# Last layer's dispatch: experts chosen in two parts, the choice in fewer operations, two gated products moved behind the logits

## The chip, the cores and the metric

The kernel runs on one core of one Trainium2 chip. Its time is the device time of one execution in microseconds; the time of a kernel is the median of its runs. The engines are TensorE (PE in the rows), VectorE (DVE), ScalarE (ACT), GpSimd (POOL) and SyncE (SP). Each works through its own list of instructions in order, and they wait for each other by semaphores.

## The reference, cut to what matters

Two layers over 4096 tokens of width 256 are computed, each an attention-like part and a mixture of experts, with a modulation by fixed vectors around them. Layer 0's mixture runs two rounds ("B0", "B1") with 6 experts of which each token takes 2; layer 1's ("D") is what the change is mostly about:

```python
h = _layernorm(x, axis=-1) * (1 + cb) + sb
# _L1_ffn_ref(h, ...), 8 experts, 2 per token
t = h * rsqrt(mean(h * h) + 1e-6) * norm_weight
gate_logits = t @ gate_w.T
gate_scores, expert_idx = top_k(gate_logits, 2)
routing_weights = softmax(gate_scores)
out = sum over the two experts of routing_weight * (gelu(t @ W1.T + B1) @ W2.T + B2)
x = x + gb * (h + out)
```

## The kernel before

The tokens are eight tiles of 512 (`NB = 8`, `CT = 4` groups of 128 rows each, 32 groups in all: `NT`). Every order below is the order in which the program text issues instructions to an engine.

**Preparation of layer 1's mixture** (`d_prep_*`). For each tile VectorE takes statistics (`d_stats_vector`, L2273 and L2277), GpSimd the inverse deviation (`rs`, a small filler L183, L2332 and a power L2334), VectorE the modulated row in two passes of four operations (`d_modulate_vector`, L2288, which does not need `rs`, and L2292, which does), ScalarE the sum of squares (`d_squares_scalar`, L2358), GpSimd the inverse root mean square (`rs2`, L183, L2342, L2344), TensorE the transposed rows (`turned`, L2393), ScalarE their copy out of PSUM (`take`, L2368, into one of two buffers `p_hT`), TensorE the logits (`logits`, L2402) and the product with the gate vector's diagonal (`gated`, L2412), VectorE the scaled logits (L2312) and the addition of the gated product to x (`d_residual_vector`, L2304), ScalarE the normalised rows (`rows`, L2376), which SyncE stores to DRAM (L2431).

VectorE works three tiles ahead: in turn t it does the modulation of tile t+3, the statistics of tile t+4, the addition of tile t-1 and the logits of tile t. GpSimd's order is rs(0), rs(1), rs(2), rs2(0), rs(3), rs2(1), rs(4), rs2(2), rs(5) and so on. `rs2(t)` has a wait of its own:

```python
if t >= 2:
    g.wait_ge(r.logits.sem, r.logits.at(t - 2))
```

because the two buffers that it writes are read by the scaled logits.

**Choice** (`routed_vector`, L952 to L987): over all 32 groups at once VectorE picks the best expert and then the second, 8 operations for the first and 10 for the second, each waiting for the one before. The second starts with three that take the first pick out of the logits (L968, L970, L972). In layer 0 the same function is used with 6 experts. The sum of the picks goes to `picked` (L2443 for layer 1, L1771 for layer 0), with a transposed write.

**Dispatch** (`dispatch_vector`, `dispatch_tensor`): TensorE counts the picks, VectorE works out each token's slot, then builds one-hot tables in four quarters (L2489 to L2492) whose product on TensorE (L2519) inverts the permutation; from it VectorE makes the row numbers for the gathers (L2495 to L2504). GpSimd then gathers rows (L2571) and scatters results (L2577) while TensorE multiplies for 39 blocks of 256 slots (L2618, L172). The one-hot tables lie where the preparation's buffers lay, so their start waits for the last gated product and the last stored rows.

**In layer 0's rounds** the second choice, `picked` and the ranks are VectorE's work between the rounding steps of the expert products (L1651, L1658, L1664, L1667), and TensorE's transposition of a later tile waits for the ranks (`COUNT_AT`).

Of the kernel before, what the change touches and what calls it, by code (L numbers as in the profile page):

```python
# [14 lines left out]
P = 128  # L15
# [936 lines left out]
def routed_vector(v, b, link, kind, which):  # L952

    E = E1 if kind == "D" else E0
    g = b.logits[:, :, 0:E]
    z, t, one, two = (x[:, :, 0:E] for x in (b.r_z, b.r_t, b.r_one, b.r_two))
    top = b.r_top[:, :]
    rank = mid(b.rank[:, 0:E], NT)
    if which == 0 and kind == "D":
        v.tensor_copy(z, g).then_inc(link.sem, 1)  # L960
        v.wait_ge(link.sem, link.next())
    elif which == 0:
        row = ROW["gb"] + (kind == "B1") * E0
        v.tensor_tensor(z, g, mid(b.rows[:, row:row + E0], NT), ALU.add).then_inc(link.sem, 1)
        v.wait_ge(link.sem, link.next())
    pick, gate = ((one, b.r_ga[:, :]), (two, b.r_gb[:, :]))[which]
# [7 lines left out]
    v.tensor_reduce(top, z, AX.X, ALU.max).then_inc(link.sem, 1)  # L974
    v.wait_ge(link.sem, link.next())
    v.tensor_tensor(t, z, spread(top, E), ALU.is_equal).then_inc(link.sem, 1)
# [7 lines left out]
    v.tensor_tensor(t, pick, g, ALU.mult).then_inc(link.sem, 1)  # L984
    v.wait_ge(link.sem, link.next())
    v.tensor_reduce(gate, t, AX.X, ALU.add).then_inc(link.sem, 1)
    v.wait_ge(link.sem, link.next())  # L987
# [1319 lines left out]
def d_prep_vector(v, b, s, r):  # L2307
# [9 lines left out]
    for t in range(NB):  # L2317
        if t + EARLY < NB:
            d_modulate_vector(v, b, r, t + EARLY)
        if t + EARLY + 1 < NB:  # L2320
            d_stats_vector(v, b, r, t + EARLY + 1)
        if t >= 1 and t + 1 < NB:
            d_residual_vector(v, b, r, t - 1)
        logits(t)


def d_prep_gpsimd(g, b, r):
# [20 lines left out]
    for t in range(NB):  # L2348
        rs2(t)
        if t + EARLY < NB:  # L2350
            rs(t + EARLY)

# [8 lines left out]
def d_prep_scalar(act, b, s, r):  # L2361
    def take(t):
        par = t % 2
        if t >= 2:
            act.wait_ge(r.gh.sem, r.gh.at(t - 2))
        for k in range(KD):
            act.wait_ge(r.hT_ps.sem, r.hT_ps.at(t, k + 1))
            act.activation(b.p_hT[par][:, k, :], b.bank[k][:, :], ACT.Copy).then_inc(r.hT.sem, 1)  # L2368
# [12 lines left out]
    for t in range(NB):  # L2381
        take(t)
        rows(t)
        if t + 2 < NB:
            d_squares_scalar(act, b, r, t + 2)


def d_prep_tensor(pe, b, r, m):
# [7 lines left out]
    def logits(t):  # L2396
# [3 lines left out]
        for c in range(CT):  # L2400
            for k in range(KD):
                ins = pe.matmul(b.bank[4 + t % 2][:, c * E1:(c + 1) * E1], b.p_hT[t % 2][:, k, c * P:(c + 1) * P], b.router["D"][:, k, :],  # L2402
                                start=k == 0, stop=k == KD - 1)
        ins.then_inc(r.logit_ps.sem, 1)

    def gated(t):
        if t >= 2:
            pe.wait_ge(r.xh.sem, r.xh.at(t - 2))
        for c in range(CT):
            for k in range(KD):  # L2410
                at = (c % 2) * D + k * P
                ins = pe.matmul(b.bank[d_sum_banks(t)[c // 2]][:, at:at + P], b.p_hT[t % 2][:, k, c * P:(c + 1) * P], b.p_diag[:, k, :], start=True, stop=True)  # L2412
            if c % 2:
                ins.then_inc(r.gh.sem, 1)
# [6 lines left out]
    for t in range(1, NB):  # L2421
        turned(t)
        gated(t - 1)
        logits(t)
    gated(NB - 1)


def d_prep_sync(sp, b, r, rows):
    for t in range(NB):
        sp.wait_ge(r.hn.sem, r.hn.at(t))  # L2430
        sp.dma_start(rows[t * TB:(t + 1) * TB, :].rearrange("(c p) n -> p c n", p=P), b.p_xn[t % 2][:, :, :]).then_inc(r.row_kept[t % 2].sem, 16)  # L2431
# [5 lines left out]
def dispatch_vector(v, b, s, link, r, E, nblk):  # L2437
# [45 lines left out]
    for par in range(2):  # L2483
        v.wait_ge(r.row_kept[par].sem, r.row_kept[par].at(NB // 2 - 1))
# [17 lines left out]
    v.tensor_scalar(b.gather_i, b.gather_i, N - 1, None, ALU.bitwise_and).then_inc(r.gather_at.sem, 1)  # L2502
    v.wait_ge(link.sem, link.next())
    v.scalar_tensor_tensor(b.scatter_i, b.source, -1.0, b.padding, ALU.add, ALU.add).then_inc(r.scatter_at.sem, 1)  # L2504


def dispatch_tensor(pe, b, r, E, nblk):
# [4 lines left out]
    pe.matmul(b.bank[1][:, 0:E * NT], b.every, flat_picked, start=True, stop=True).then_inc(r.counted.sem, 1)  # L2512
    for j in range(4):
# [759 lines left out]
```

## Time and profile before

| | |
|---|---|
| median of 3 runs | 1962.32 us (1961.79 to 1965.76) |
| profiled execution | 1967.77 us, its span 1965.8 us |
| busy: TensorE, VectorE, ScalarE, GpSimd | 1747.9, 1392.4, 1026.4, 783.0 us |
| mean granted clock of TensorE over the span | 0.949 of full |
| preparation of layer 1's mixture, from the last addition of the part before to the last scaled logits | 1588.0 to 1628.7 us |
| choice and dispatch, to the first gather | 1628.8 to 1660.3 us |
| products of the 39 blocks | 1667.7 to about 1910 us |

Times in rows count from the start of the span. A row of the timeline has the start, the time from the first instruction's start to the last one's end, engine, line, operation, what is written and read, how many, and in brackets the idle time before it with what ended that. Instructions of an engine overlap by some 0.07 to 0.1 us, so the distance of two starts is what an operation costs in a row of operations.

### The profile page before, as it was taken

What the parts mean: (1) busy time and instruction counts of PE and PEld (TensorE: products, weight loads), DVE (VectorE), ACT (ScalarE), POOL (GpSimd) and SP (SyncE); (2) the same over time, 40 slices, a digit from 0 to 9 for tenths busy, and PEclk for the clock granted to TensorE, in tenths of its full rate; (3) what the DMA queues carried; (4) which work ended last, traced back from release to release, by engine and by line L of the source; (5) the groups of instructions that cost most, each with busy time, mean ns of one, the idle gap of its engine ahead of it and who ended that gap; (6) DMA issues with size and microseconds to landing.
All of it is one profiled execution on the core that took longest, in us unless ns stands there. A gap on an engine that the chain in (4) does not pass through costs nothing.

```text
span 1965.8 us, 31803 instructions
## 1 busy us (share of the span) xinstructions
PE 1747.9 (89%) x11154; PEld 1543.5 (79%) x11154; DVE 1392.4 (71%) x2536; ACT 1026.4 (52%) x2052; POOL 783.0 (40%) x860
## 2 busy tenths in 40 slices
PE   5999999999999999999969999999289984999990
PEld 4788888888888878888858788888166784999990
DVE  4665465465445788777758887777699897788876
ACT  4344344334322434555546446554488653888882
POOL 2132232232222101777731037777222041788840
PEclk9899999999998999999978999999699986999995
DMA  4200000000012430666753326666710013788948
GB/s 161 65 1 12 11 0 11 11 11 0 11 58 65 129 126 20 205 198 193 204 185 118 116 63 208 191 197 172 232 65 1 1 63 139 255 268 271 275 166 267
DMA packets 147128, 233.00 MB, mean 119 GB/s; under 512 B 28226, under 2 KB 103236, under 8 KB 142020
## 3 DMA queue, kind: packets, MB, share of 16 engines
q1 hardware_dynamic: 123396, 167.04, 26.2%
q0 software_dynamic: 23616, 64.52, 11.1%
q8 instruction: 60, 0.98, 0.2%
q14 instruction: 56, 0.46, 0.1%
HBM read 175.65 MB, written 55.33 MB: 117 GB/s over the span
## 4 chain that ended last, share of the span: by engine, by line
PE 62%; issue 13%; DVE 13%; POOL 6%; ACT 3%; DMA 2%; SPq 0%; POOLq 0%; DVEq 0%; ACTq 0%
PE bank L172 42%; PE bank L2179 4%; PE bank L1310 3%; PE bank L432 2%; PE bank L450 1%; POOL a_aTm L920 1%; PE bank L1319 1%; POOL d_got L2571 1%; POOL a_xa L905 1%; PE bank L2618 1%; PE bank L1230 1%; POOL a_rs L164 1%; DVE d_back L2768 1%; PE bank L239 1%; PE bank L475 1%
## 5 line engine op out<-in xcount | busy, mean ns | idle before, releaser
L1865 POOL DMA_INDIRECT got<-b_rows,b_gather_i x168 | 170.5, 1015 | 215.5 <-PE bank L1310 164.9
L183 POOL TENSOR_TENSOR spare_g<-neg_half 128x1 f32<-128x1 f32 x80 | 20.9, 262 | 579.1 <-ACT a_sg L563 142.5
L172 PE MATMUL bank<-gT_hi,w_hi 128*128 128x512 f32 x592 | 246.5, 416 | 0.8 <-DVE gT_lo L1651 0.8
L172 PE MATMUL bank<-gT_hi,w_lo 128*128 128x512 f32 x592 | 237.1, 401 | 0.0
L172 PE MATMUL bank<-gT_lo,w_hi 128*128 128x512 f32 x592 | 236.9, 400 | 0.0
L1651 DVE TENSOR_TENSOR gT_lo<-bank,gT_hi 128x512 fp32r<-128x512 f32 x148 | 97.3, 690 | 134.2 <-ACT gT_hi L1453 106.2
L1483 ACT ACTIVATE m_hi<-gs 128x512 fp32r<-128x512 f32 x116 | 73.0, 633 | 121.8 <-DVE gs L1658 67.5
L172 PE MATMUL bank<-w_hi,m_hi 128*128 128x256 f32 x464 | 130.7, 282 | 5.2 <-DVE sent L1680 5.2
L172 PEld LDWEIGHTS bank<-gT_hi,w_lo 128*128 128x128 f32 x592 | 113.1, 191 | 27.9
L172 PEld LDWEIGHTS bank<-gT_hi,w_hi 128*128 128x128 f32 x592 | 113.8, 192 | 22.0 <-DVE gT_lo L1651 0.9
L172 PEld LDWEIGHTS bank<-gT_lo,w_hi 128*128 128x128 f32 x592 | 114.1, 193 | 21.5
L172 PE MATMUL bank<-w_lo,m_hi 128*128 128x256 f32 x464 | 130.6, 281 | 0.0
L172 PE MATMUL bank<-w_hi,m_lo 128*128 128x256 f32 x464 | 130.4, 281 | 0.0
L2571 POOL DMA_INDIRECT d_got<-d_rows,d_gather_i x78 | 92.9, 1191 | 60.7 <-DVE d_gather_i L2502 37.2
L2577 POOL DMA_INDIRECT d_kept<-d_sent,d_scatter_i x78 | 97.6, 1251 | 47.6 <-DVE d_sent L2735 26.6
L920 POOL TENSOR_TENSOR a_aTm<-a_aT,masks 128x512 f32<-128x512 f32 x56 | 71.3, 1285 | 108.5 <-PE bank L432 83.9
L1474 ACT ACTIVATE gs<-bank,w_cols 128x512 f32<-128x512 f32 x84 | 57.6, 688 | 95.8 <-PE bank L172 95.8
L1872 POOL DMA_INDIRECT b_kept<-sent,b_scatter_i x88 | 90.3, 1026 | 35.2 <-issue 26.2
L602 ACT ACTIVATE a_ax<-bank 128x512 f32<-128x512 f32 x48 | 28.6, 597 | 127.4 <-PE bank L432 127.4
L172 PE MATMUL bank<-d_gT_hi,v_hi 128*128 128x256 f32 x312 | 92.9, 298 | 1.8 <-DVE d_gT_lo L2715 1.8
L172 PEld LDWEIGHTS bank<-w_hi,m_hi 128*128 128x128 f32 x464 | 87.9, 189 | 7.9 <-issue 5.5
L172 PE MATMUL bank<-v_hi,d_m_hi 128*128 128x256 f32 x312 | 91.2, 292 | 1.4 <-issue 0.9
(465 smaller groups left out, 5650.9 us busy)
## 6 DMA issues: line engine op xcount, KB each, us to landing
v_raw<-in_units SPq DMA_DIRECT2D x39, 1024.0 KB, 5.0
w_raw<-in_units SPq DMA_DIRECT2D x56, 256.0 KB, 3.8
shared<-in_units SPq DMA_DIRECT2D x40, 256.0 KB, 4.1
b_rows<-x SPq DMA_DIRECT2D x16, 512.0 KB, 3.1
got<-b_rows SPq DMA_DIRECT2D x16, 512.0 KB, 4.5
d_back<-d_kept SPq DMA_DIRECT2D x16, 512.0 KB, 8.9
close_back<-b_kept SPq DMA_DIRECT2D x14, 512.0 KB, 8.8
w_raw<-b_folded SPq DMA_DIRECT2D x26, 256.0 KB, 4.3
```

Source lines behind the costliest of these rows:

```text
L172: ins = pe.matmul(out, a, b, start=first and n == 0, stop=last and n == of - 1)
L432: ins = pe.matmul(B[1][:, chunk(c)], b.aTm[l % 2][:, chunk(c)], b.xx[:, chunk(c)], start=True, stop=True)
L920: g.tensor_tensor(four(b.aTm[l % 2][:, :]), four(b.aT[:, :]), mid(b.maskT[:, l, :], CT), ALU.mult).then_inc((s.aTm if l else s.aTm0).sem, 1)
L1310: ins = pe.transpose(B[6 + f][:, c * P:(c + 1) * P], src(c, f), b.ident)
L1474: act.activation(product_of(b, st)[:, o, :], B[2 + o][:, :], ACT.Silu, bias=b_bias(b, st, 1, o)).then_inc(r.sg.sem, 1)
L1483: act.activation(b.m_hi[st.par][:, o, :], b.gs[:, o, :], ACT.Copy).then_inc(r.m_hi.sem, 1)
L1651: v.tensor_tensor(b.gT_lo[st.par][:, f, :], B[6 + f][:, :], f32(b.gT_hi[st.par][:, f, :]), ALU.subtract).then_inc(r.gT_lo.sem, 1)
L1865: g.indirect_dma_start(b.got[:, kg % 4, c, :], None, dram.rows[rnd], bass.IndirectOffsetOnAxis(b.gather_i[:, q:q + 1], 0)).then_inc(r.gath ...
L1872: g.indirect_dma_start(dram.kept[rnd], bass.IndirectOffsetOnAxis(b.scatter_i[:, q:q + 1], 0), b.sent[kg % SENDS][:, c, :], None).then_inc( ...
L2179: ins = pe.matmul(out, a, w, start=n == 0, stop=last and n == len(lhs) - 1)
L2571: g.indirect_dma_start(b.got[n % 6][:, c, :], None, rows, bass.IndirectOffsetOnAxis(b.gather_i[:, q:q + 1], 0)).then_inc(landed.sem, 16)
L2577: g.indirect_dma_start(kept, bass.IndirectOffsetOnAxis(b.scatter_i[:, q:q + 1], 0), b.sent[k % 4][:, c, :], None).then_inc(r.scattered[k % ...
```

## The change

1. `routed_vector` works on a range of groups. For layer 1 it takes the best value straight from the logits (no copy) and keeps it as the score, so that the product and the sum that fetched the score fall away; the three operations that mask the first pick become one. Layer 1: 5 and 6 operations in place of 8 and 10. Layer 0: 8 and 8 in place of 8 and 10.
2. Layer 1 chooses for groups 0 to 23 (`ROUTED_FIRST`) after tile 5's logits, then scales the logits of tiles 6 and 7, then chooses for groups 24 to 31.
3. `picked` is written straight and its two inputs are read transposed, in both layers.
4. TensorE turns tiles 6 and 7 and makes both logits before the gated product of tile 5; the gated products of tiles 6 and 7 come after the counts. A third buffer `p_hT` is added; tile 7's gated product goes to PSUM banks 4 and 5. ScalarE takes tiles 6 and 7 before it writes the normalised rows of either.
5. VectorE's additions of tiles 4 and 5 move into the dispatch, those of tiles 6 and 7 behind the index work; TensorE waits for the last of them before its first transposition of gathered rows.
6. GpSimd's order becomes rs2(0), rs2(1), rs(3), rs2(2), rs(4), rs2(3), rs(5), rs2(4), rs(6), rs2(5), rs(7), rs2(6), rs2(7). The wait in `rs2` stays.
7. The rows are stored one row further on (the last one at row 0), with three transfers for tile 7, so that the gather's row number needs no addition; the index work reads PSUM directly and gives the gather's numbers after three operations. The inversion uses PSUM bank 0. The softmax's first three operations (`gates_vector`) move ahead of the wait for the inversion.

```diff
@@ routed_vector
+    n = t1 - t0
+    most = gate if kind == "D" else top
     if which == 0 and kind == "D":
-        v.tensor_copy(z, g).then_inc(link.sem, 1)
-        v.wait_ge(link.sem, link.next())
+        z = g
...
-    if which == 1:
-        v.tensor_scalar(t, one, -2.0, 1.0, ALU.mult, ALU.add).then_inc(link.sem, 1)
+    else:
+        v.scalar_tensor_tensor(z, one, -BIG, g if kind == "D" else z, ALU.mult, ALU.add).then_inc(link.sem, 1)
         v.wait_ge(link.sem, link.next())
-        v.tensor_scalar(t, t, BIG, None, ALU.mult).then_inc(link.sem, 1)
...
-        v.tensor_tensor(z, z, t, ALU.min).then_inc(link.sem, 1)
...
+    if kind != "D":
+        v.tensor_tensor(t, pick, g, ALU.mult).then_inc(link.sem, 1)
         v.wait_ge(link.sem, link.next())
+        v.tensor_reduce(gate, t, AX.X, ALU.add).then_inc(link.sem, 1)
         v.wait_ge(link.sem, link.next())
@@ picked_vector and dispatch_vector
-    v.tensor_tensor(b.picked.rearrange("p e t -> p t e"), one, two, ALU.add).then_inc(r.picked.sem, 1)
+    v.tensor_tensor(b.picked, one.rearrange("p t e -> p e t"), two.rearrange("p t e -> p e t"), ALU.add).then_inc(r.picked.sem, 1)
@@ d_prep_vector
-    for t in range(NB):
+    for t in range(NB - 2):
...
-        if t >= 1 and t + 1 < NB:
+        if 1 <= t < NB - 3:
             d_residual_vector(v, b, r, t - 1)
         logits(t)
+    v.wait_ge(r.logits.sem, r.logits.at(NB - 3))
+    for which in range(PICKS):
+        routed_vector(v, b, link, "D", which, 0, ROUTED_FIRST)
+    logits(NB - 2)
+    logits(NB - 1)
+    v.wait_ge(r.logits.sem, r.logits.at(NB - 1))
+    for which in range(PICKS):
+        routed_vector(v, b, link, "D", which, ROUTED_FIRST, NT)
@@ d_prep_gpsimd
-    for t in range(NB):
+    for t in range(2):
         rs2(t)
+    for t in range(NB - 2):
         if t + EARLY < NB:
             rs(t + EARLY)
+        rs2(t + 2)
@@ d_prep_scalar
-    for t in range(NB):
+    for t in range(NB - 2):
         take(t)
         rows(t)
-        if t + 2 < NB:
-            d_squares_scalar(act, b, r, t + 2)
+        d_squares_scalar(act, b, r, t + 2)
+    for t in (NB - 2, NB - 1):
+        take(t)
+    for t in (NB - 2, NB - 1):
+        rows(t)
@@ d_gated_tensor, the function gated before
+    if t == NB - 1:
+        pe.wait_ge(r.logits.sem, r.logits.at(t))
+    elif t >= 2:
+        pe.wait_ge(r.xh.sem, r.xh.at(t - 2))
@@ d_prep_tensor
-    for t in range(1, NB):
+    for t in range(1, NB - 2):
         turned(t)
-        gated(t - 1)
+        d_gated_tensor(pe, b, r, t - 1)
         logits(t)
-    gated(NB - 1)
+    turned(NB - 2)
+    pe.wait_ge(r.hT.sem, r.hT.at(NB - 2))
+    turned(NB - 1)
+    logits(NB - 2)
+    logits(NB - 1)
+    d_gated_tensor(pe, b, r, NB - 3)
@@ dispatch_vector
-    d_residual_vector(v, b, r, NB - 2)
+    d_residual_vector(v, b, r, NB - 4)
...
-    d_residual_vector(v, b, r, NB - 1)
+    d_residual_vector(v, b, r, NB - 3)
+    gates_vector(v, b, s, link, "D")
     v.wait_ge(r.inverse.sem, r.inverse.at(0))
-    v.tensor_copy(b.found, b.bank[2][:, 0:2 * nq]).then_inc(link.sem, 1)
-    v.wait_ge(link.sem, link.next())
-    v.scalar_tensor_tensor(b.source, b.found[:, 0:nq], float(P), b.found[:, nq:2 * nq], ALU.mult, ALU.add).then_inc(link.sem, 1)
-    v.wait_ge(link.sem, link.next())
-    v.tensor_scalar(b.gather_i, b.source, float(N - 1), None, ALU.add).then_inc(link.sem, 1)
+    at, part = b.bank[0][:, 0:nq], b.found[:, 0:nq]
+    v.tensor_copy(part, b.bank[0][:, nq:2 * nq]).then_inc(link.sem, 1)
+    v.wait_ge(link.sem, link.next())
+    v.scalar_tensor_tensor(b.gather_i, at, float(P), part, ALU.mult, ALU.add).then_inc(link.sem, 1)
+    v.wait_ge(link.sem, link.next())
+    v.tensor_scalar(b.gather_i, b.gather_i, N - 1, None, ALU.bitwise_and).then_inc(r.gather_at.sem, 1)
...
+    for t in (NB - 2, NB - 1):
+        d_residual_vector(v, b, r, t)
@@ dispatch_tensor
+    d_gated_tensor(pe, b, r, NB - 2)
+    d_gated_tensor(pe, b, r, NB - 1)
@@ d_prep_sync
+    sp.dma_start(turned_rows(t * TB + 1, end * P), b.p_xn[t % 2][:, 0:end, :]).then_inc(r.last_rows.sem, 16)
+    sp.dma_start(rows[N - P + 1:N, :], b.p_xn[t % 2][0:P - 1, end, :]).then_inc(r.last_rows.sem, 16)
+    sp.dma_start(rows[0:1, :], b.p_xn[t % 2][P - 1:P, end, :]).then_inc(r.last_rows.sem, 16)
@@ d_tensor
+    pe.wait_ge(r.xh.sem, r.xh.at(NB - 1))
     turn(0)
```

## Rows read from the trace of the kernel before

**Rows 1.** The page's chain that ended last, shares of the span by engine.
```profile
PE 62%; issue 13%; DVE 13%; POOL 6%; ACT 3%; DMA 2%; SPq 0%; POOLq 0%; DVEq 0%; ACTq 0%
```

**Rows 2.** Timeline of VectorE, preparation of layer 1's mixture.
```profile
1596.43 0.16 DVE L2312 TENSOR_TENSOR logits<-bank,p_rs 128x32 f32<-128x32 f32 x1
...
1598.35 1.67 DVE L2292 SCALAR_TENSOR_TENSOR pd_h<-pd_h,p_rs,mod 128x256 f32<-128x256 f32 x4
...
1602.85 0.18 DVE L2312 TENSOR_TENSOR logits<-bank,p_rs 128x32 f32<-128x32 f32 x1
...
1604.53 1.67 DVE L2292 SCALAR_TENSOR_TENSOR pd_h<-pd_h,p_rs,mod 128x256 f32<-128x256 f32 x4
...
1618.45 1.28 DVE L2304 TENSOR_TENSOR x<-x,bank 128x512 f32<-128x512 f32 x2
...
1628.55 0.19 DVE L2312 TENSOR_TENSOR logits<-bank,p_rs 128x32 f32<-128x32 f32 x1 [4.21 <-PE bank L2402]
```

**Rows 3.** Timeline of VectorE, layer 1's choice and the start of its dispatch.
```profile
1628.78 0.29 DVE L960 COPY r_z<-logits 128x256 f32<-128x256 f32 x1
...
1636.62 1.27 DVE L2443 TENSOR_TENSOR d_picked<-r_one,r_two 128x256 bf16<-128x256 f32 x1
1637.52 1.48 DVE L2304 TENSOR_TENSOR x<-x,bank 128x512 f32<-128x512 f32 x2
...
1642.58 0.60 DVE L2469 TENSOR_TENSOR d_where<-r_one,d_rank_of 128x256 f32<-128x256 f32 x1
```

**Rows 4.** Timeline of VectorE, end of layer 1's dispatch.
```profile
1656.23 1.28 DVE L2304 TENSOR_TENSOR x<-x,bank 128x512 f32<-128x512 f32 x2
1658.33 0.32 DVE L2495 COPY d_found<-bank 128x156 f32<-128x156 f32 x1 [0.82 <-PE bank L2519]
...
1659.23 0.20 DVE L2502 TENSOR_SCALAR d_gather_i<-d_gather_i 128x78 int32<-128x78 int32 x1
```

**Rows 5.** Timeline of TensorE, layer 0's first round: a transposition behind the ranks.
```profile
726.24 1.97 PE L1310 MATMUL bank<-ident,got 128*128 128x128 f32 x8 [2.59 <-DVE b_rank_of L1785]
```

**Rows 6.** Timeline of VectorE, layer 0's first round: second choice, then rounding.
```profile
714.56 0.25 DVE L968 TENSOR_SCALAR r_t<-r_one 128x192 f32<-128x192 f32 x1
...
715.14 0.36 DVE L972 TENSOR_TENSOR r_z<-r_z,r_t 128x192 f32<-128x192 f32 x1
...
718.27 1.05 DVE L1771 TENSOR_TENSOR b_picked<-r_one,r_two 128x192 bf16<-128x192 f32 x1
718.93 1.50 DVE L1651 TENSOR_TENSOR gT_lo<-bank,gT_hi 128x512 fp32r<-128x512 f32 x2
```

**Rows 7.** Timeline of ScalarE: the last tile taken out of PSUM.
```profile
1624.70 1.08 ACT L2368 ACTIVATE pd_hT<-bank 128x512 f32<-128x512 f32 x2 [1.00 <-PE bank L2393]
```

**Rows 8.** Timeline of TensorE: last tile's turn and logits, first gathered rows.
```profile
1623.97 1.07 PE L2393 MATMUL bank<-ident,pd_h 128*128 128x128 f32 x8
...
1626.67 1.85 PE L2402 MATMUL bank<-router_D,pd_hT 128*128 128x8 f32 x16
...
1664.41 1.11 PE L2618 MATMUL bank<-ident,d_got 128*128 128x128 f32 x4 [6.11 <-DMA d_got<-d_rows,d_gather_i]
```

**Rows 9.** Timeline of GpSimd, preparation of layer 1's mixture: filler and power of three groups.
```profile
1596.59 0.19 POOL L183 TENSOR_TENSOR spare_g<-neg_half 128x1 f32<-128x1 f32 x1 [9.32 <-DVE p_mv L2277]
...
1597.19 1.12 POOL L2334 TENSOR_TENSOR p_rs<-p_rs,neg_half 128x4 f32<-128x4 f32 x1
...
1603.36 0.52 POOL L183 TENSOR_TENSOR spare_g<-neg_half 128x1 f32<-128x1 f32 x1
...
1604.35 1.12 POOL L2344 TENSOR_TENSOR p_rs<-p_rs,neg_half 128x4 f32<-128x4 f32 x1
...
1619.97 0.19 POOL L183 TENSOR_TENSOR spare_g<-neg_half 128x1 f32<-128x1 f32 x1 [2.16 <-ACT pd_sq L2358]
...
1620.51 1.01 POOL L2344 TENSOR_TENSOR p_rs<-p_rs,neg_half 128x4 f32<-128x4 f32 x1
```

**Rows 10.** Busy times by stretch, layer 0; after the five engines: granted clock, DMA, GB/s.
```profile
720.00:730.00 10.00, 7.20 (x30) 5.62 (x29) 9.15 (x22) 4.10 (x7) 0.00 (x0) 0.83 0.11 32
```

More of the change, by code:

```diff
@@ L945, in a_gpsimd, with routed_vector @@
     residual(NB - 1)
-def routed_vector(v, b, link, kind, which):
+def routed_vector(v, b, link, kind, which, t0=0, t1=NT):
     E = E1 if kind == "D" else E0
[L955 to L958, printed above, removed]
+    n = t1 - t0
+    g = b.logits[:, t0:t1, 0:E]
+    z, t, one, two = (x[:, t0:t1, 0:E] for x in (b.r_z, b.r_t, b.r_one, b.r_two))
+    top = b.r_top[:, t0:t1]
+    rank = mid(b.rank[:, 0:E], n)
+    pick, gate = ((one, b.r_ga[:, t0:t1]), (two, b.r_gb[:, t0:t1]))[which]
+    most = gate if kind == "D" else top
     if which == 0 and kind == "D":
-        v.tensor_copy(z, g).then_inc(link.sem, 1)
-        v.wait_ge(link.sem, link.next())
+        z = g
     elif which == 0:
         row = ROW["gb"] + (kind == "B1") * E0
-        v.tensor_tensor(z, g, mid(b.rows[:, row:row + E0], NT), ALU.add).then_inc(link.sem, 1)
+        v.tensor_tensor(z, g, mid(b.rows[:, row:row + E0], n), ALU.add).then_inc(link.sem, 1)
         v.wait_ge(link.sem, link.next())
-    pick, gate = ((one, b.r_ga[:, :]), (two, b.r_gb[:, :]))[which]
-    if which == 1:
-        v.tensor_scalar(t, one, -2.0, 1.0, ALU.mult, ALU.add).then_inc(link.sem, 1)
+    else:
+        v.scalar_tensor_tensor(z, one, -BIG, g if kind == "D" else z, ALU.mult, ALU.add).then_inc(link.sem, 1)
         v.wait_ge(link.sem, link.next())
-        v.tensor_scalar(t, t, BIG, None, ALU.mult).then_inc(link.sem, 1)
-        v.wait_ge(link.sem, link.next())
-        v.tensor_tensor(z, z, t, ALU.min).then_inc(link.sem, 1)
-        v.wait_ge(link.sem, link.next())
-    v.tensor_reduce(top, z, AX.X, ALU.max).then_inc(link.sem, 1)
+    v.tensor_reduce(most, z, AX.X, ALU.max).then_inc(link.sem, 1)
     v.wait_ge(link.sem, link.next())
-    v.tensor_tensor(t, z, spread(top, E), ALU.is_equal).then_inc(link.sem, 1)
+    v.tensor_tensor(t, z, spread(most, E), ALU.is_equal).then_inc(link.sem, 1)
     v.wait_ge(link.sem, link.next())
@@ L2401, in logits @@
             for k in range(KD):
-                ins = pe.matmul(b.bank[4 + t % 2][:, c * E1:(c + 1) * E1], b.p_hT[t % 2][:, k, c * P:(c + 1) * P], b.router["D"][:, k, :],
+                ins = pe.matmul(b.bank[4 + t % 2][:, c * E1:(c + 1) * E1], b.p_hT[t % TURNED][:, k, c * P:(c + 1) * P], b.router["D"][:, k, :],
                                 start=k == 0, stop=k == KD - 1)
         ins.then_inc(r.logit_ps.sem, 1)
[L2406 to L2414, printed above, removed]
     pe.wait_ge(r.router.sem, r.router.at(0))
@@ L2442, in dispatch_vector @@
     by_expert = lambda ap: ap.rearrange("p (e t) -> p e t", e=E)
-    v.tensor_tensor(b.picked.rearrange("p e t -> p t e"), one, two, ALU.add).then_inc(r.picked.sem, 1)
+    v.tensor_tensor(b.picked, one.rearrange("p t e -> p e t"), two.rearrange("p t e -> p e t"), ALU.add).then_inc(r.picked.sem, 1)
     earlier, tile = b.bank[0][:, 0:E * NT], b.bank[1][:, 0:E * NT]
-    d_residual_vector(v, b, r, NB - 2)
+    d_residual_vector(v, b, r, NB - 4)
     v.wait_ge(r.counted.sem, r.counted.at(0))
@@ L3095, in vector_d @@
         def vector_d(v, link):
-            d_prep_vector(v, bD, s, rd)
-            v.wait_ge(rd.logits.sem, rd.logits.at(last))
-            for which in range(PICKS):
-                routed_vector(v, bD, link, "D", which)
+            d_prep_vector(v, bD, s, link, rd)
             dispatch_vector(v, bD, s, link, rd, E1, NBD)
-            gates_vector(v, bD, s, link, "D")
             shares_vector(v, bD, s, link, "D")
```

45 lines of the change are left out of this document (28 added, 17 removed).

## The prediction

> **What bounds the kernel now.** I read the page's chain first: TensorE holds 62% of it and VectorE 13% [rows 1]. That is the whole span; the change touches three short places, so I read each engine's timeline there. In layer 1's preparation VectorE is the bound. The reader should see in [rows 2] that each turn's work starts where the last one's ended, and that bracketed waits appear only behind the last tile (4.21 us before the last scaled logits, which wait for TensorE). From there to the first gather one dependent chain on VectorE sets the time: choice, `picked`, slots, one-hot tables, index work [rows 3, 4]. After that the expert blocks follow the gathers at a fixed pace, so what the gathers gain I carry one to one to the end. In layer 0's rounds TensorE bounds nearly everything, except where the second choice sits: there it waits 2.59 us for a rank that VectorE makes late [rows 5].
>
> **The preparation without any new wait.** Both kernels finish modulating tile 7 at 1618.45 [rows 2]. `picked` starts at 1636.62 [rows 3], 18.2 us later. After the change two paths run from that moment. VectorE: the addition of tile 3 (1.2), two scaled logits (0.25), the choice for 24 groups, two more scaled logits (0.3). An operation on 192 elements costs (718.27 - 715.14) / 8 = 0.39 us [rows 6], eleven cost 4.3; together 6.05. ScalarE and TensorE: the last square (0.6, my estimate), tile 6 out of PSUM (1.0) [rows 7], tile 7 turned (1.0), two tiles of logits (3.5) [rows 8]; tile 7's copy lies beside tile 6's logits. Together 6.1, so the two are balanced. Then one scaled logits (0.2) and eleven operations on 64 elements. The 18 operations of the old choice took 7.84 [rows 3], 0.436 each with three short ones in them; a full one is 0.455, so 64 elements are worth 0.065 and a 64-element operation is estimated at 0.39 - 2 x 0.065 = 0.26: 2.8 us. `picked` would start 9.1 us after 1618.45 in place of 18.2: **9.1 us gained**. The additions of tiles 4 to 7 leave this path; where they go is priced below.
>
> **The new wait: GpSimd's order.** Before, rs(t+3) starts when the statistics are done, before the scaled logits of tile t-1. Now rs2(t+1) stands ahead of it, and rs2(t+1) waits for the scaled logits of tile t-1, because its two buffers alternate. So from turn 1 on GpSimd can't begin rs(t+3) until VectorE has finished turn t-1 altogether, and must do two groups; VectorE has just the first pass of the modulation (1.5 us) to do meanwhile, then it waits for rs(t+3). The queue behind it is everything: statistics, additions, logits. This happens four times, for tiles 4 to 7. A GpSimd group takes 1.55 us when it meets nothing (1619.97 to 1621.52), 1.72 beside the first pass (1596.59 to 1598.31), and 2.11 in the longest case (1603.36 to 1605.47) [rows 9]. From the end of the scaled logits to the second pass was 1603.03 to 1604.53 = 1.50 [rows 2]. It becomes 0.08 + 1.72 + 1.55 = 3.35, a stall of 1.85; with 2.11 for the first group 3.7 and a stall of about 2.2. For tile 4, where rs was already late (1596.59 to 1598.35 = 1.76 [rows 2]), it is 1.6 to 1.95. Sum 7.15 to 8.55; I take **7.5 lost**, near the row with the same alignment. The preparation keeps 1.6 of its 9.1.
>
> What a pass of VectorE adds to a GpSimd group beside it is 0.17 to 0.56 us for the three instructions together [rows 9], where one operation of the pass takes 0.4. The Trainium skill ("SBUF — State Buffer", section "Who interferes with whom") says that a VectorE instruction with two SBUF inputs, as these have, and a GpSimd instruction that reads SBUF lock each other out of a shared pair of ports for a whole instruction. By the row the stall is 1.85; held to the letter, with the pass running without a gap, it would be that of the rival below who is locked out.
>
> **TensorE's clock.** TensorE idles in each turn for VectorE's additions, and the stalls lengthen that idle time by some 1.9 us. In layer 0, after a wait of 2.59 us, eight transpositions took 1.97 us [rows 5] against 1.07 at full clock [rows 8], and the granted clock of that stretch is 0.83, a mixture of the 1.2 and 2.4 GHz levels [rows 10]. If the same happens here, the turn of tile 7 costs 0.9 more and the logits some 0.4: 0 to 1.3, and the last gated product, at twice its time, could make the one-hot tables wait 0.75 more. Bound 0 to 2.05; I take **0.5 lost**. At full clock the gated products of tiles 6 and 7 (2 us each, from the counts on) end before the tables start, some 8 us after `picked`.
>
> **`picked` and the addition behind it.** `picked` occupied VectorE for 0.90 (1636.62 to 1637.52), and the addition's end at 1639.0 released the scan, 2.38 after the start [rows 3]. An operation of this size with one transposed input took 0.60 [rows 3]; with two I bound it at 0.60 to 0.8. The addition (now of tile 4, ready for long) costs its usual 1.25. That gives 1.85 to 2.05, so 0.35 to 0.55 gained; I take **0.45**.
>
> **Index work.** From 1658.33 to 1659.43 [rows 4] it took 1.10 to the gather's numbers. Now: half the copy (0.28), one combined operation into the integers (0.27), the mask (0.20) = 0.75, estimates from the neighbours in that chain. **0.35 gained.** In front of it VectorE now has the addition of tile 5 (1.2) and the three operations of the gates (0.65) from 1656.23 on: 1658.1, just under the inversion at 1658.33, so free; if TensorE were faster there, this would be the bound.
>
> **What is hidden.** The additions of tiles 6 and 7 start after the gather's and scatter's numbers and take 2.4 us; TensorE's new wait for them ends about 1662.2 on the old clock of events, the first gathered rows are turned at 1664.41 [rows 8]. Cover 2.2 us; without it TensorE's first product would be late by the rest. The softmax shares and the first weights' rounding move 2 us later with it and still precede the first turned rows. The rows of tile 7 are written by ScalarE some 5 us later than before and stored by three transfers in place of one; the tables wait for them some 10 us later. SyncE's next work, the experts' weights, waits for VectorE's dispatch in any case. GpSimd's gathers are behind the same wait. ScalarE has idle time throughout. Extra buffer: nothing.
>
> **Layer 0.** The second choice loses two operations, 714.56 to 715.14 = 0.58 for the two short ones [rows 6] (the remaining one costs the same), and `picked` occupied 0.66 there; with reads transposed I expect 0.46 to 0.65. The rounding for TensorE stands right behind both [rows 6], and the chain runs on VectorE up to the rank that ends TensorE's 2.59 us wait. So each round gains 0.5 to 0.8, I take 0.68: **1.35 for the two**.
>
> **Sum.** -9.1 + 7.5 + 0.5 - 0.45 - 0.35 - 1.35 = -3.25 us. The profiled execution is 1967.77 with a span of 1965.8, which would become 1964.5 and 1962.55; the median of the runs shown is 1962.32, 5.45 lower, and the sum goes to it: 1962.32 - 3.25 = **1959.1**. The likeliest case's own range by the bounds: -9.1 + 7.15 - 0.55 - 0.35 - 1.6 = -4.45 to -9.1 + 8.55 + 2.05 - 0.35 - 0.35 - 1.0 = -0.2, so 1957.9 to 1962.1.
>
> **Rivals.**
> *No stall.* rs2's wait releases early enough, or ScalarE's earlier release shortens something I count as fixed, and the preparation gives its full 9.1. Then -9.1 - 0.45 - 0.35 - 1.35 = -11.25: 1951.1. For it: GpSimd is idle most of the time, and the old order made ScalarE wait for rs2. Against it: the wait is in the code, and VectorE, not ScalarE, has no gaps [rows 2]. Chance 0.10.
> *GpSimd locked out (slower).* If rs2's operations can't run beside VectorE's first pass, both groups follow it: 1.58 + 1.55 + 1.55 = 4.7, a stall of 3.2 each, 12.8 in all in place of 7.5: the sum is +2.05, 1964.4. Break-even is at 2.7 a turn, slower by over 0.2% at 3.7. For it: group times of 2.11 beside such a pass [rows 9]. Against it: that is the worst of them, and it is 0.6 above the undisturbed one. Chance 0.10. (The Trainium skill's rule on the shared ports, "SBUF — State Buffer", would bring it about.)
> *Layer 0 gives nothing.* TensorE's waits there end by something else that comes last. Then 1960.5. For it: the expert rounds are TensorE's elsewhere. Against it: no gap on VectorE from the choice to the rank. Chance 0.05.
> The likeliest: 0.75.
>
> **Chances and range.** A measurement of this kernel can tell some 0.2% (3.9 us) from no change, so the lines are 1958.4 and 1966.2. Of the likeliest case's 0.75, 0.23 lies under 1958.4, 0.03 comes out slower by an unpriced loss. Faster 0.23 + 0.10 = 0.33, slower 0.03 + half of the lock-out case 0.05 = 0.08, within 0.59. The range takes in the lock-out and leaves out the case without stall: 1955.0 to 1964.5.
>
> **What the new profile would show.** Right: four waits of VectorE before L2292's successor with GpSimd's power as releaser, 1.5 to 2.3 us each; GpSimd's rs2 starting right at the end of scaled logits; some 11 + 11 choice operations, the first eleven 0.39 apart; `picked` under 0.8; the first gather some 3 us earlier relative to the span, 1.35 of it already there when layer 1's preparation starts. Wrong: no such waits (then 1951), waits above 2.7 (then slower), the scaled logits of tile 7 waiting for TensorE by more than 1 us, the tables waiting for the last gated product or the last rows, or the first turned rows waiting for VectorE's last addition.

## The result, and the profile after

The change makes the kernel slower by a little: 1970.9 us (1968.25 to 1972.46, 8 runs) against 1967.03 for the kernel before (1961.79 to 1970.87, 8 runs that include the three shown above). The ratio is 1.0023, with a 95% interval of 1.0013 to 1.0033: +4.5 us by the ratio where -3.25 was forecast. The median of before was 4.7 us higher in the eight runs than in the first three, so the forecast counts as a difference: it would be 1963.8 on this base.

The profiled execution of after took 1968.25 us, span 1966.3, mean granted clock 0.944. The profiled executions differ by a few us before the code differs at all (the first choice of layer 0 starts at 705.20 here, 2.3 us earlier than before), so a span by itself says little. I read stretches between two events instead. From the end of the product that makes `p_diag` (the start of layer 1's preparation) to the first gather, the kernel before takes 68.64 us and the one after 73.47. The forecast for that stretch was -1.9 (-9.1 + 7.5 + 0.5 - 0.45 - 0.35); it is **+4.83**.

The shares in the page's chain hardly move, as in [rows 1]:

```profile
PE 62%; issue 13%; DVE 12%; POOL 7%; ACT 3%; DMA 2%; SPq 1%; POOLq 0%; DVEq 0%; ACTq 0%
```

The timeline of VectorE in the preparation, after (for [rows 2, 3]):

```profile
1594.65 1.67 DVE L2290 SCALAR_TENSOR_TENSOR pd_h<-pd_h,p_rs,mod 128x256 f32<-128x256 f32 x4 [2.02 <-POOL p_rs L2346]
...
1602.92 1.67 DVE L2290 SCALAR_TENSOR_TENSOR pd_h<-pd_h,p_rs,mod 128x256 f32<-128x256 f32 x4 [2.02 <-POOL p_rs L2346]
...
1621.05 1.28 DVE L2305 TENSOR_TENSOR x<-x,bank 128x512 f32<-128x512 f32 x2
...
1627.01 0.36 DVE L979 TENSOR_TENSOR r_two<-r_t,r_top 128x192 f32<-128x192 f32 x1
1630.58 0.19 DVE L2316 TENSOR_TENSOR logits<-bank,p_rs 128x32 f32<-128x32 f32 x1 [3.21 <-PE bank L2431]
1633.93 0.19 DVE L2316 TENSOR_TENSOR logits<-bank,p_rs 128x32 f32<-128x32 f32 x1 [3.17 <-PE bank L2431]
...
1636.99 0.62 DVE L2473 TENSOR_TENSOR d_picked<-r_one,r_two 128x256 bf16<-128x256 f32 x1
```

Two things are to be seen. The second pass of the modulation waits 2.02 us for GpSimd's power; the two further ones, at 1611.19 and 1619.46, wait 2.02 as well. And VectorE, done with the first part of the choice at 1627.4, waits twice, 3.21 and 3.17 us, for TensorE's logits. Behind them the kernel is as forecast: 3.06 us from the last scaled logits to `picked`.

The same stretch on TensorE, after (for [rows 8]):

```profile
1602.87 1.07 PE L2422 MATMUL bank<-ident,pd_h 128*128 128x128 f32 x8
1607.55 3.75 PE L2412 MATMUL bank<-pd_diag,pd_hT 128*128 128x128 f32 x16 [3.61 <-DVE x L2305]
1611.12 1.87 PE L2431 MATMUL bank<-router_D,pd_hT 128*128 128x8 f32 x16
1612.85 1.07 PE L2422 MATMUL bank<-ident,pd_h 128*128 128x128 f32 x8
1615.82 3.78 PE L2412 MATMUL bank<-pd_diag,pd_hT 128*128 128x128 f32 x16 [1.91 <-DVE x L2305]
1619.40 3.42 PE L2431 MATMUL bank<-router_D,pd_hT 128*128 128x8 f32 x16
1622.67 1.95 PE L2422 MATMUL bank<-ident,pd_h 128*128 128x128 f32 x8
1625.31 1.97 PE L2422 MATMUL bank<-ident,pd_h 128*128 128x128 f32 x8 [0.69 <-ACT pd_hT L2381]
1627.06 6.83 PE L2431 MATMUL bank<-router_D,pd_hT 128*128 128x8 f32 x32
```

and busy times by stretch, after (the column behind the five engines is the granted clock):

```profile
1607.00:1611.00 4.00, 3.45 (x16) 3.45 (x17) 2.18 (x6) 1.32 (x4) 2.96 (x6) 0.50 0.02 4
1611.00:1619.00 8.00, 6.09 (x41) 5.86 (x41) 6.21 (x20) 4.23 (x14) 2.84 (x7) 0.71 0.19 66
1619.00:1634.00 15.00, 14.31 (x68) 13.91 (x68) 7.36 (x21) 7.93 (x22) 3.18 (x7) 0.50 0.28 96
```

TensorE runs at the lower of its two levels, 1.2 GHz, from 1615.82 to the end of the preparation, and everything costs nearly double: the gated product 3.78 for 2.05, a tile's logits 3.42 for 1.85, a turn 1.97 for 1.07. In the kernel before the granted clock is 1.00 from 1600 to 1629.

On GpSimd, after, the order reads as forecast (for [rows 9]): the group of rs2 stands behind the scaled logits, and rs behind it.

```profile
1607.74 0.30 POOL L183 TENSOR_TENSOR spare_g<-neg_half 128x1 f32<-128x1 f32 x1 [4.85 <-DVE logits L2316]
...
1608.52 1.13 POOL L2356 TENSOR_TENSOR p_rs<-p_rs,neg_half 128x4 f32<-128x4 f32 x1
...
1610.15 1.01 POOL L2346 TENSOR_TENSOR p_rs<-p_rs,neg_half 128x4 f32<-128x4 f32 x1
```

The end of the dispatch, VectorE, after (for [rows 4]): the addition, the three operations of the gates (the last one is shown), the copy of half the table, and two operations that write integers.

```profile
1656.18 1.27 DVE L2305 TENSOR_TENSOR x<-x,bank 128x512 f32<-128x512 f32 x2
...
1657.82 0.19 DVE L994 TENSOR_TENSOR r_gb<-r_gb,r_top 128x32 f32<-128x32 f32 x1
1657.93 0.23 DVE L2528 COPY d_found<-bank 128x78 f32<-128x78 f32 x1
...
1658.47 0.20 DVE L2532 TENSOR_SCALAR d_gather_i<-d_gather_i 128x78 int32<-128x78 int32 x1
```

Layer 0's wait for the rank, TensorE, after (for [rows 5]):

```profile
723.36 1.70 PE L1308 MATMUL bank<-ident,got 128*128 128x128 f32 x8 [2.33 <-DVE b_rank_of L1783]
```

### The profile page after: what moved, and what is told of

The parts are those of the page before. It is cut to its first block, busy times and chain, and to the rows that moved or that the text cites. A ratio compares the mean times of both kernels' runs of the same rounds, so it can differ in the third digit from the quotient of the medians.

```text
span 1966.3 us, 31808 instructions
## 1 busy us (share of the span) xinstructions
PE 1753.2 (89%) x11154; PEld 1550.3 (79%) x11154; DVE 1389.5 (71%) x2536; ACT 1027.1 (52%) x2052; POOL 785.0 (40%) x860
## 4 chain that ended last, share of the span: by engine, by line
PE 62%; issue 13%; DVE 12%; POOL 7%; ACT 3%; DMA 2%; SPq 1%; POOLq 0%; DVEq 0%; ACTq 0%
PE bank L172 42%; PE bank L1308 3%; PE bank L2177 3%; PE bank L432 2%; POOL d_got L2608 2%; POOL a_aTm L920 1%; PE bank L450 1%; PE bank L1317 1%; POOL a_xa L905 1%; PE bank L1228 1%; POOL a_rs L164 1%; PE bank L2656 1%; DVE d_back L2807 1%; PE bank L483 1%; PE bank L239 1%
## 5 line engine op out<-in xcount | busy, mean ns | idle before, releaser
L1870 POOL DMA_INDIRECT b_kept<-shared,b_scatter_i x80 | 82.9, 1036 | 24.4 <-issue 24.4
```

The lines of the kernel that those rows point to most:

```text
L1870: g.indirect_dma_start(dram.kept[rnd], bass.IndirectOffsetOnAxis(b.scatter_i[:, q:q + 1], 0), b.sent[kg % SENDS][:, c, :], None).then_inc( ...
```

## The experiments

My theory after the result: two losses, each in its own place. GpSimd's order makes VectorE stall four times (8.1 us), and TensorE's clock takes most of what the two-part choice should have given. The rival on the first is that the stalls are only moved waits; on the second, that the clock falls because of the stalls alone, and the tail's own order is innocent. "Prep to gather" below is the stretch from `p_diag` to the first gather, "tile 7" the time from the end of tile 7's modulation to its scaled logits, both from the profiled execution, so one execution of each kernel. The differences of the stretch to the kernel before agree with those of the ratio to within 1.8 us in all eleven kernels.

| kernel | ratio to before | 95% interval | prep to gather | tile 7 |
|---|---|---|---|---|
| before | 1 | | 68.64 | 10.10 |
| after | 1.0023 | 1.0013 to 1.0033 | 73.47 | 12.88 |
| gpsimd_order_back | 0.9985 | 0.9975 to 0.9995 | 64.73 | 12.34 |
| four_rs2_buffers | 0.9973 | 0.9963 to 0.9983 | 63.36 | 10.97 |
| filler_matmuls | 1.0025 | 1.0016 to 1.0034 | 74.89 | 14.29 |
| small_filler | 0.9993 | 0.9984 to 1.0002 | 68.82 | 8.20 |
| old_order_last_filler | 0.9961 | 0.9948 to 0.9974 | 61.16 | 8.76 |
| four_buffers_and_filler | 0.9959 | 0.9946 to 0.9972 | 61.16 | 8.78 |
| gated_product_between_turns | 0.9966 | 0.9954 to 0.9978 | 60.19 | 7.77 |
| before_new_gpsimd_order | 1.0056 | 1.0042 to 1.0069 | 79.53 | 13.40 |
| before_layer0_choice | 0.9995 | 0.9984 to 1.0005 | 68.68 | 10.10 |
| before_choice_and_picks | 0.9978 | 0.9967 to 0.9989 | 64.68 | 10.11 |

**The stalls: `gpsimd_order_back`.** The kernel after with the old order on GpSimd.

```diff
-    for t in range(2):
-        rs2(t)
-    for t in range(NB - 2):
-        if t + EARLY < NB:
-            rs(t + EARLY)
-        rs2(t + 2)
+    for t in range(NB):
+        rs2(t)
+        if t + EARLY < NB:
+            rs(t + EARLY)
```

> The changed kernel with GpSimd's old order (rs2 of tile t, then rs of tile t+3); all else as changed. My theory: the new order makes VectorE wait four times 2.0 us, and the gaps that this opens on TensorE let its clock fall to half, which doubles the turn and the logits of the last two tiles. Both should go: no wait of VectorE for GpSimd above 0.3 us in the preparation, granted clock at or near 1.0 from there to the last scaled logits, 6 to 7 us from the end of tile 7's modulation to its scaled logits in place of 12.9, the time 12 to 16 us under the changed kernel, ratio to before about 0.993 to 0.996. Rival 1, the stall alone matters and the clock falls for the moved gated products: the waits are gone, but the last logits still take 3.4 us each, ratio about 0.998. Rival 2, neither matters because the loss lies behind the first gather: ratio stays near 1.002.

All four waits are gone, and the kernel becomes 7.5 us faster than after (0.9985 against 1.0023). But tile 7 still takes 12.34, where 6 to 7 and a ratio of 0.993 to 0.996 were expected: what came is the expectation's first rival, the waits gone and the logits still slow. TensorE, in this kernel:

```profile
1616.80 1.07 PE L2420 MATMUL bank<-ident,pd_h 128*128 128x128 f32 x8
1620.05 1.97 PE L2420 MATMUL bank<-ident,pd_h 128*128 128x128 f32 x8 [2.18 <-ACT pd_hT L2379]
1621.81 6.83 PE L2429 MATMUL bank<-router_D,pd_hT 128*128 128x8 f32 x32
```

Tile 6 is turned at full clock; then TensorE waits 2.18 us for ScalarE, and the turn and both logits run at half. So the clock falls without any stall.

**The other way to undo them: `before_new_gpsimd_order`.** The kernel before with nothing but the new loop of GpSimd.

> The kernel before with only GpSimd's order as in the change. My theory: four waits of VectorE of 1.6 to 2.1 us, together 7.5 to 8.2 us, and on top what the clock costs in that kernel's tail, where gated products and logits alternate: 2 to 5 us. Time 9 to 13 us over before, ratio 1.005 to 1.0065. If the clock matters only in the changed order of TensorE: 8 us, ratio 1.004. Rival, that ScalarE gains by the earlier rs2 what VectorE loses: ratio 1.000 to 1.002.

VectorE shows the same four waits of 2.02 us, and the kernel loses 11 us, as expected: 8.1 for the stalls and 3.3 at tile 7 (13.40 for 10.10), less 0.6 between `picked` and the first gather. TensorE's clock falls twice here. Behind a wait of 3.31 us it is low, and back to full before tile 5 is turned; behind a wait of 1.66 us it is low again, and this second time it delays the last tiles:

```profile
1598.90 3.78 PE L2414 MATMUL bank<-pd_diag,pd_hT 128*128 128x128 f32 x16 [3.31 <-DVE x L2304]
...
1612.70 1.07 PE L2395 MATMUL bank<-ident,pd_h 128*128 128x128 f32 x8
1615.43 3.78 PE L2414 MATMUL bank<-pd_diag,pd_hT 128*128 128x128 f32 x16 [1.66 <-DVE x L2304]
1619.01 3.42 PE L2404 MATMUL bank<-router_D,pd_hT 128*128 128x8 f32 x16
```

The order is thus a loss in either kernel, and it isn't a wait that was there anyway.

**The stalls without the old order: `four_rs2_buffers`.** Four buffers for rs2, so that it waits for the logits four tiles back; GpSimd keeps its new order.

```diff
+        b.p_rs2 += [sb(after_a, f"p_rs2{i}", [P, CT]) for i in (2, 3)]
...
-        if t >= 2:
-            g.wait_ge(r.logits.sem, r.logits.at(t - 2))
+        if t >= 4:
+            g.wait_ge(r.logits.sem, r.logits.at(t - 4))
```

(and `b.p_rs2[t % 4]` wherever it is written or read)

> The changed kernel with four buffers for the inverse root mean squares in place of two, so that rs2 of tile t waits for the scaled logits of tile t-4, not t-2; GpSimd's new order stays. My theory, that the wait on the scaled logits makes the stalls: none of the four waits of 2.0 us is left, and because rs2 comes early here, ScalarE is not late at tile 6 either (with the old order it reached tile 6 some 3 us after the modulation of tile 7, TensorE idled 2.2 us and did the last turn and both logits at half clock). So 6 to 8 us from the end of tile 7's modulation to its scaled logits, and the preparation gives the 9.1 us of the forecast's rival without stall: time 10 to 12 us under before, ratio 0.994 to 0.995. If the clock falls in the last two tiles for their own order (both logits behind a wait for a copy, no gated products between): waits gone, last logits 3.4 us each, ratio 0.997 to 0.9985, as with the old order.

It was the shared buffer, not the order as such, that made the stall. ScalarE gets tile 6 earlier too, and TensorE's last wait shrinks from 2.18 to 0.80. Even then the clock falls, and the expected 6 to 8 us for tile 7 and ratio of 0.994 to 0.995 did not come; the expectation's other case did (the waits gone, the last logits at 3.4 us a tile, 0.9973):

```profile
1618.73 1.07 PE L2422 MATMUL bank<-ident,pd_h 128*128 128x128 f32 x8
1620.60 1.97 PE L2422 MATMUL bank<-ident,pd_h 128*128 128x128 f32 x8 [0.80 <-ACT pd_hT L2381]
1622.36 6.84 PE L2431 MATMUL bank<-router_D,pd_hT 128*128 128x8 f32 x32
```

**The clock alone: `filler_matmuls` and `small_filler`.** The kernel after, stalls and all, with products of two identity matrices, whose result nobody reads, ahead of the turns of tiles 2 to 6. In the first kernel 20 ahead of tiles 2 to 5 and 12 ahead of tile 6, in the second 8 and 4. A row counts two for each such product (x16 for eight), as it does for the gated product and the logits.

```diff
+    def filler(n):
+        for _ in range(n):
+            pe.matmul(b.bank[0][:, 0:P], b.ident, b.ident, start=True, stop=True)
...
+        if t >= 2:
+            filler(20)
         turned(t)
...
+    filler(12)
     turned(NB - 2)
```

> The changed kernel with 20 products of the identity with itself in front of each turn of tiles 2 to 5 and 12 in front of tile 6's, into a PSUM bank that the turn then overwrites: work added, no wait removed. It separates the clock from the stalls. If the clock is the larger part of what I mis-sized: the four waits of 2.0 us stay, granted clock stays near 1.0, turn of tile 7 about 1.0 and the logits 1.8 us each, 6 to 7 us from the end of tile 7's modulation to its scaled logits, the time 5 to 7 us under the changed kernel, ratio to before about 0.999. If the clock falls whatever TensorE does, or the logits are slow for another reason: no gain, ratio 1.002 or more.

> The changed kernel with GpSimd's new order and smaller fillers: 8 identity products in front of each turn of tiles 2 to 5, 4 in front of tile 6's. The first filler run used 20 and 12, which took 4.7 and 2.9 us, more than the gaps, and made TensorE late. Clock theory: the four waits of 2.0 us stay, the last logits take 3.6 us together, 7 to 8 us from the end of tile 7's modulation to its scaled logits instead of 12.9, time 4 to 5 us under the changed kernel, ratio to before 1.000. If the gaps that remain still let the clock fall: ratio 1.002, logits 6.8 us.

The first missed its expected gain and settled only half of the question. The clock stayed full (the two tiles of logits took 3.64), but the dummy products took 4.71 us, longer than the idle time that they were to fill, and TensorE fell behind: 1.0025. The second tells it: the four stalls of 2.02 us stay, tile 7 falls from 12.88 to 8.20, and the ratio from 1.0023 to 0.9993. The logits took 5.58 there in place of the expected 3.6. TensorE had no gap from the start of tile 7's turn (1625.21) to their end, and yet its granted clock was 1.00 up to 1626, 0.87 from there to 1628 and 0.50 from 1628 to 1632: it fell in the middle of unbroken work.

**The last tiles' clock: `old_order_last_filler` and `four_buffers_and_filler`.** Eight such products only, ahead of tile 6's turn, in the two kernels without stalls.

```diff
+    filler(8)
     turned(NB - 2)
```

> The changed kernel with GpSimd's old order and 8 products of the identity in front of the turn of tile 6 (work added: about 1.9 us at full clock, inside TensorE's idle time of 2.2 us before the turn of tile 7). The run with the old order alone took 12.3 us from the end of tile 7's modulation to its scaled logits, with 6.83 us for the two tiles' logits. If the half clock is what costs there: granted clock 1.0 through the last logits, 3.6 us for both, 4 to 5 us gained over the old order alone, ratio to before about 0.996. If the logits are slow for another reason: 6.8 us stay, ratio 0.9985.

> The kernel after with four p_rs2 buffers (no stall) and, in addition, eight identity products on TensorE before tile 6 is turned. Theory (the stalls and the clock are the two losses and are separable): with the buffers alone tile 7's turn took 1.97 us after an idle time of 0.80 and the two tiles of logits 6.84. The eight products cost TensorE 1.9 us there, because nothing is idle before tile 6's turn; with the clock full behind them the turn takes 1.1 and the logits 3.7, so tile 7's scaled logits come about 2.0 us earlier than with the buffers alone: ratio to before 0.996, from the end of tile 7's modulation to its scaled logits 8.7 to 9.0 us instead of 10.9. Rival (the clock falls by itself in this part): turn 1.97 and logits 6.8 stay, the products are pure cost, ratio 0.998.

In the first, tile 7 falls from 12.34 to 8.76 and the ratio from 0.9985 to 0.9961, with intervals that don't touch: the wait of 2.18 us becomes 0.80, since the eight products fill the rest of it, the turn takes 1.09 for 1.97 and the logits 3.64 for 6.83, as expected. This is the clearest of the experiments on the clock. TensorE in the second:

```profile
1615.84 2.03 PE L2437 MATMUL bank<-ident 128*128 128x128 f32 x16
1617.70 1.04 PE L2422 MATMUL bank<-ident,pd_h 128*128 128x128 f32 x8
1619.54 1.10 PE L2422 MATMUL bank<-ident,pd_h 128*128 128x128 f32 x8 [0.80 <-ACT pd_hT L2381]
1620.47 3.64 PE L2431 MATMUL bank<-router_D,pd_hT 128*128 128x8 f32 x32
1623.96 3.50 PE L2412 MATMUL bank<-pd_diag,pd_hT 128*128 128x128 f32 x16
```

The wait for ScalarE is the same 0.80 us as in `four_rs2_buffers`, and yet the turn behind it takes 1.10 instead of 1.97. The wait alone does not set the clock; what TensorE did before it does too. The products put the fall off rather than prevent it: the gated product right behind the logits took 3.50 us for some 2, with no wait in front of it. But there it no longer delays the logits. Two us of useless work, on the path, gain 2.2 us at tile 7; the 0.14% in the ratio lies within the two intervals. The expectation on `four_buffers_and_filler` held in each number.

**Real work in the gap: `gated_product_between_turns`.** `four_rs2_buffers` with the change's own move undone for tile 5: its gated product stands between the turns of tiles 6 and 7 instead of behind both logits.

```diff
     turned(NB - 2)
+    d_gated_tensor(pe, b, r, NB - 3)
     pe.wait_ge(r.hT.sem, r.hT.at(NB - 2))
     turned(NB - 1)
     logits(NB - 2)
     logits(NB - 1)
-    d_gated_tensor(pe, b, r, NB - 3)
```

> The kernel after with four p_rs2 buffers, and tile 5's gated product put back between the turns of tiles 6 and 7 instead of behind both tiles of logits. It is real work in the place of the 0.80 us in which TensorE waits for ScalarE. Theory (idle time of TensorE sets its clock): the product takes 2.05, tile 7's turn starts about 1.1 us later but at full clock (1.07 for 1.97) and the logits take 3.6 for 6.84: tile 7's scaled logits come 2.8 us earlier than with the buffers alone, ratio to before 0.9958, and no dummy work is needed. Rival (the clock falls by itself in this part): the product takes 3.75, turn and logits stay at 1.97 and 6.8, the scaled logits come 2.8 us later than with the buffers alone, ratio 0.9987.

```profile
1618.65 1.07 PE L2422 MATMUL bank<-ident,pd_h 128*128 128x128 f32 x8
1619.56 2.01 PE L2412 MATMUL bank<-pd_diag,pd_hT 128*128 128x128 f32 x16
1621.41 1.04 PE L2422 MATMUL bank<-ident,pd_h 128*128 128x128 f32 x8
1622.28 3.64 PE L2431 MATMUL bank<-router_D,pd_hT 128*128 128x8 f32 x32
```

Putting 2 us of work ahead of the critical turn brings tile 7's logits 3.2 us earlier (7.77 for 10.97), the shortest tile 7 of all (2.8 us expected), because the wait is filled and the turn and logits behind it run at full clock. In the whole time it gives 0.07%, with intervals that overlap those of `four_rs2_buffers`; the trace's stretch from prep to gather, 60.19 for 63.36, is where it is seen. The expected 0.9958 lies within the interval. It can't be told apart from the version with dummy products either.

**The parts that were cheap: `before_layer0_choice` and `before_choice_and_picks`.** The kernel before with the new `routed_vector` and the new `picked` in layer 0 alone, and then in both layers (over all 32 groups at once in layer 1), and nothing else.

> The kernel before with the new choice and the new write of the picks in layer 0's two rounds only; layer 1 as before. The forecast had 0.68 us a round, 1.35 in all: ratio 0.9993. The two profiles, aligned at the first choice, differ by 3.3 us at the start of layer 1's preparation: if that comes from this part, ratio 0.9983. If TensorE's waits there end by something else: ratio 1.0000.

> The kernel before with the new choice and the new write of the picks in both layers, and nothing else: one choice over all 32 groups, old orders on every engine, old index work. Sum by parts: layer 0 1.35 by the forecast (1.0 measured, uncertain by 2), layer 1's choice 7.84 us to 11 x 0.455 = 5.0, 2.8 gained, picks and addition 0.5: 4.3 to 4.7 us, ratio 0.9977. Rival, that a shorter VectorE chain here is covered by something else (the last stored rows, TensorE's last gated product): ratio 0.9993 or more.

Layer 0 gives 1 us, not distinguishable from nothing; with layer 1 it is 4.3 us. The fewer operations and the cheaper `picked` alone are worth half of what the best version of the whole change is worth (8.1 us at 0.9959), without touching one order.

The expectation on `before_layer0_choice` asks where 3.3 us come from: from the first choice of layer 0 to the end of the product that makes `p_diag` the kernel before takes 884.15 us and the one after 880.83. Layer 0's change doesn't explain it. Alone it shows 883.87, and the eight other kernels with it 883.4 to 884.0; `before_new_gpsimd_order`, whose layer 0 is that of the kernel before, shows 880.48. So this difference appears without any difference in the code, and its cause stays open; the stretch from prep to gather does not hold it.

## Why the prediction was wrong, step by step

**The step that failed is the clock.** I took 0.5 us for it and a bound of 2.05. Measured from the end of tile 7's modulation, its turn starts 4.26 us later (forecast 1.6: square and copy, with tile 6 already turned), its logits 1.75 after that (1.0), and its scaled logits 6.87 after that (3.5): 12.88 for 6.1, so **6.8 us**, more than three times the bound. All three come from the clock. Worked out from the rows: at full clock the gated product of 1615.82 and the logits behind it would have ended 3.3 us earlier, tile 6 would have been turned before tile 7 was modulated, and the rest is the plain doubling of a turn and two logits. `small_filler`, with the same four stalls and full clock up to tile 7's turn, confirms it: that turn starts 1.66 us after the modulation and the logits 0.92 after it, as forecast, and only the logits are slow. My row was right ([rows 5], 1.97 us behind a wait); the error was to carry over only that one step and to put "some 0.4" for two tiles of logits, as if the clock came back after one turn. Doubling each of them, from [rows 5, 8], would have given 0.9 + 2 x 1.6 = 4.1 and a forecast of no change; the backlog in front makes up the rest. So the preparation's gain up to `picked` was 2.2 us (18.17 to 15.94), not 9.1.

The 9.1 was a little too high for a kernel without stalls, too. It took tile 6 as turned when tile 7's modulation ends. In `four_rs2_buffers` tile 6's turn starts only 0.47 us after it and tile 7's 2.34 us after it, at full clock until then; in the kernel before, tile 6's turn starts 0.47 after it as well (1618.92 against the 1618.45 of [rows 2]). With the stalls TensorE has the time, so this 0.7 us does not count in the kernel as changed.

The Trainium skill ("TensorE: Matmul & The Clock Gate", section "HAM oscillation — how this bites in real kernels") describes a kernel that waits between bursts of products and starts each burst at the lower clock. By that rule the first half-clock product after a long wait was to be expected, and the trace agrees (3.75 us behind 3.61 us of waiting). The page's kernel waits 3 to 5 us each time; here the clock was also low behind waits of 1.91 and 0.80 us.

**The stall was right.** Forecast four, 1.6 to 2.2 us each, 7.5 in all; measured four times 2.02, 8.1. The first group takes 1.91 beside VectorE's pass (1.85 was built on 1.72), the second 1.54. GpSimd was not locked out by that pass: the lock-out rival wanted 3.2 a turn. Nor did the case without stall come about; `four_rs2_buffers` shows what would have brought it, though with only half of its 11.25 us (5.3 by the ratio), since the clock fell there as well.

**But the stalls cost more than their own length.** Four kernels take the two losses apart: with stalls 1.0023, and 0.9993 with fillers (which keep the clock only in part); without stalls 0.9973, and 0.9959 with a filler. Removing the stalls alone gives 9.8 us, the small fillers alone 5.9, both changes 12.6. So the two overlap by some 3 us. In the stretch from prep to gather the same sum gives 10.1 + 4.7 - 12.3 = 2.5; each ratio is uncertain by some 2 us, so the overlap itself is not clear of noise. That the clock still falls when the stalls are gone is clear (0.9985 and 0.9961 in the old order, without and with the eight products).

**Choice, `picked` and the addition.** Operations on 192 elements are 0.39 apart, on 64 elements 0.26 apart, as estimated. From `picked` to the scan 1.74 us, for 2.29 before: 0.55 gained (0.45 forecast, its upper bound).

**Index work.** 0.7 us less from the start of the addition in front of it to the first gather, 3.32 for 4.02 (0.35 forecast); the stretch from the scan to that addition is 0.13 longer. The other half is the named risk the other way round: the product that inverts the permutation was quicker, 1.29 us for 1.87, at a granted clock of 0.99 for 0.71 (1656 to 1659), and the addition and the gates became the bound, with the copy right behind them.

**Layer 0.** TensorE's wait fell by 0.26 us and the ranks came 0.62 earlier in round 0; alone it is 1.0 us by the ratio against 1.35, within the interval, which takes in nothing as well.

**Behind the first gather** I expected no change; the profiled execution shows 306.8 us for 305.55. GpSimd's fourth gather took 1.37 us for 0.94, beside VectorE's rounding of the weights, which now lies there; the seventh took 1.21 for 1.52. But nine other kernels, with either form of that code, show 304.88 to 306.76 for the same stretch (`before_new_gpsimd_order` alone 307.63), so 1.25 us is no finding. What was called hidden (last rows, one-hot tables, first turned rows) was hidden: no wait shows there.

Sum of the measured terms: -9.1 + 6.8 + 8.1 - 0.55 - 0.7 = +4.55 up to the gather (4.83 in the trace); with layer 0's -1.0 and the 1.25 behind it the trace's 4.83 becomes +5.1, and the ratio says +4.5, its interval +2.6 to +6.5.

## What to carry to other kernels

When work is moved off an engine that is sometimes idle, price the engine's clock with it: double every operation of that engine from the first wait that grows up to the result that others wait for, and take that as the bound, not one instruction's surcharge. Here unbroken work did not bring the clock back before that result. A product that seems to be in the way of the critical one may be what lets it run fast; fill the wait with it first and move it only if it is longer than wait and doubling together. And before an order is changed on a helper engine, look at the waits inside the moved step: here two buffers more made the new order free (26.83 us from `p_diag` to the end of the modulation of tile 7, for 26.84 before). Whether one would have done was not tried.

## What the runs showed of the hardware

- No length of wait by itself tells the clock behind it. Full clock: behind 1.50 us in the kernel before, 1.67 in the one after, 1.78 in `small_filler`, 0.80 with eight products ahead. Half clock: behind 1.91 in the kernel after, 1.66 in `before_new_gpsimd_order`, and in `four_rs2_buffers` behind 1.42 (a gated product of 3.51 us at 1602.80) and 0.80.
- The clock can stay low under steady work, and it can fall in it. In `four_rs2_buffers` TensorE was busy for all 10 us from 1622 to 1632 at a granted clock of 0.50; in `small_filler` the clock fell between 1626 and 1628 with no gap. What makes it fall there stays open. In the kernel after, from 1615.82 to 1622.67 TensorE had no gap and stayed at half, and it was busy 14.31 of 15 us from 1619 on at a granted clock of 0.50; behind the wait at 1607.55 it was back to full after one gated product of 3.75 us.
- Products with 8 columns cost nearly what those with 128 columns do: a row of sixteen in 1.85 us against 2.05 at full clock, 3.42 against 3.78 at half.
- Reading two inputs transposed costs VectorE less than writing the output transposed: `picked` occupied it for 0.54 us in layer 1 (0.90 before) and 0.50 in layer 0 (0.66).
